# Involution on one core: products 7 and 8 of each image joined to X by transfers of their own, and the first experts' results counted exactly

## Chip, cores and metric

One core of a Trainium2 chip. The metric is device microseconds for one execution of the whole program. Three runs of the kernel before gave a median of 1173.37 us.

## The reference, cut to what matters

The program is a stack of a binary convolution, a mixture of 8 experts (two a token), an involution and a mixture of 16 experts (eight a token, with a capacity), with norms and residuals between them, on 16 images of 128 channels and 32 x 32 pixels. Two parts are touched.

The first experts (`_L0_ffn_ref`): for each token the two chosen experts, weighted and summed.

```python
for e in range(E):
    h = jax.nn.relu(x_flat @ W1[e] + b1[e])
    y = h @ W2[e] + b2[e]
    out = out + combine[:, e:e + 1] * y
```

The involution (`_L1_conv_ref`): nine taps; each is a weight per pixel, grown from the image, times the image shifted by that tap; the nine products are summed, and the sum is added to x.

```python
xv = d4_1x1(x, w_v)
pats = unfold_patches(xv, k).reshape(b, G, gc, 8, k * k, h, w)
out = (wv * pats).sum(axis=4)
...
x = x + _L1_conv_ref(_ln_c(x), ...)
```

## The kernel before

Everything is hand-scheduled: each engine has its program, written in the order in which it runs, and engines meet by semaphores alone. No planner sets an order. Phases end with all engines having reached the end of their block; a new block begins on all of them together.

**First experts** (`experts0`, lines 424 to 674). Tokens are sorted by their pair of experts into tiles of 128 rows (`SLOT`). How many tiles there are is known only at run time: VectorE works it out in `later_tables` (line 1078) and writes it to `env.totals`, and engines load it into a register with `count` (line 454). For a tile, TensorE turns the rows, multiplies them up to the 512 hidden values of each expert of the pair (line 526 and the two behind it) and down again (lines 544 to 546, eight matmuls a tile in each); ScalarE takes the rectified values in float16 (line 592), VectorE their rest (line 638). VectorE writes the result of a tile into one of 8 buffers (`OUTS`, line 658), with the token numbers beside it, and GpSimd sends it off with an indirect transfer (`send`, line 487, the transfer itself at line 489). GpSimd sends in groups of 8, so up to 7 sends behind the last real result have no rows: VectorE gives them token numbers out of bounds (line 672), for which nothing is written. The first 24 sends stand among the scatters of line 1140. The first tile begins with `take(0)` on VectorE (line 633), behind `later_tables` in VectorE's program.

**Involution** (`phase_involution`, line 1511). The images are taken one after the other; the passes of images 0, 1 and 12 to 15 are written out, those of images 2 to 11 are a loop of two (`images`, line 1553). Within a pass on image n, TensorE grows the weights of tap k into one of two PSUM buffers (`tap`, lines 1688 and 1689, four matmuls of 512 columns a tap), and among the taps it runs the steps of images n+1 and n+2: the kernels and values of the next image (lines 1669 and 1673), the group mean (1678), the turn of the rows that the first experts left (1652), the centering (1659) and the variance (1664). VectorE multiplies each grown tap by the shifted image in `product` (line 1882). Products 0 to 6 go to buffers from which GpSimd sums them with six adds (line 1628); that sum is then added to X in place by an accumulating transfer which GpSimd issues (`join_pool`, line 1616). Product 7 goes to a buffer, product 8 stays in PSUM, VectorE adds the two (`add_pair`, line 1890), and a second accumulating transfer adds this sum to X (`join_own`, line 1621); GpSimd issues it in the next image's pass, behind that image's third add. Both transfers of an image write the same part of X, so the second waits for the landing of the first:

```python
def join_own(n, q):
    pool.wait_ge(S["summed"], n * OWN_ADDS + OWN_ADDS)
    wait_apart(pool, S["pool_joined"], n * 16 + 16, env.passed)
    pool.dma_start(image(X, n), flat(own_sum[q]), accum_op=ALU.add).then_inc(S["own_joined"], 16)
```

SyncE reloads the rows of a later image (line 1569) and stores a finished image (line 1581), in turn, the store waiting for `own_joined`. VectorE's product k of an image waits until GpSimd's add k of the image before has read its buffer.

**The way into the last experts.** The choice of experts for the first two images runs on VectorE (`select`, lines 1398 to 1417), then `join_last` adds the last image's own sum to X (line 1922), then `weigh` (lines 1422 to 1432) waits for the ranks that TensorE counts. GpSimd adds its sum to the last image (line 1639), behind `join_last`, and then casts the spread weights (line 1248), which TensorE needs for the last experts.

## Time and profile before

| | |
|---|---|
| runs | 1169.5, 1173.37, 1174.52 us |
| profiled execution | 1174.4 us, span 1172.6 us, granted TensorE clock 0.958 |
| busy over the span | TensorE 1024.1, VectorE 904.3, ScalarE 778.9, GpSimd 566.7 us |
| first experts | from about 320 to 773.6 us of the span |
| involution | 773.6 to about 1084 us |
| last experts | from there to 1172.6 us |

All times in a timeline are microseconds from the first instruction of the span. A row of it gives the start, the duration, the engine, the line, the operation with output and inputs, and in brackets how long the engine had been idle and whose work ended that. An engine name with a q is its queue: an issue, or work of its sequencer. Rows of one line that follow each other are merged, with their number behind the x. "ps" is PSUM; XN, WT, Y and X are the large buffers in SBUF.

### The profile page before, as it was taken

The numbers are of one execution on the slowest core, as the hardware profiler recorded it, in microseconds if no ns is written. First come the engines' busy times: TensorE is split into PE (matmuls) and PEld (weight loads), VectorE is DVE, ScalarE is ACT, GpSimd is POOL, SyncE is SP. The second block draws the span as 40 slices with busy tenths as digits, with TensorE's granted clock in tenths as the row PEclk, the third lists the DMA queues.
The fourth block names the chain that finished last, engine by engine and source line by source line (L and its number), as shares of the span: only waits on it lengthen the run. The fifth ranks groups of instructions, "written<-read, shape, count | busy, mean of one in ns | idle before, by whom it ended". The sixth has DMA issues, their size and how long they took to land. (4 is left out here: it accounts for less than half of the span.)

```text
span 1172.6 us, 34488 instructions
## 1 busy us (share of the span) xinstructions
PE 1024.1 (87%) x9800; PEld 707.4 (60%) x9800; DVE 904.3 (77%) x2105; ACT 778.9 (66%) x2031; POOL 566.7 (48%) x442
## 2 busy tenths in 40 slices
PE   7957698898499999999999999837999999997498
PEld 2322254444299999999999999813434434433364
DVE  4669768878667777777787787706999999997687
ACT  6866399998467777777777777626656666663275
POOL 0014127657646533333333333355789889899100
PEclk9989899999789999999999999969999999999599
DMA  7200023321223211111111111121554464443000
GB/s 229 71 0 0 3 86 107 98 74 49 63 70 101 75 47 46 48 45 46 41 42 40 40 44 42 39 82 36 147 118 105 114 142 109 108 108 90 20 1 37
DMA packets 64928, 80.98 MB, mean 69 GB/s; under 512 B 10362, under 2 KB 50958, under 8 KB 64705
## 3 DMA queue, kind: packets, MB, share of 16 engines
q1 hardware_dynamic: 51552, 46.93, 13.9%
q0 software_dynamic: 13280, 32.73, 11.1%
q8 instruction: 66, 1.08, 0.4%
q14 instruction: 30, 0.24, 0.1%
HBM read 36.57 MB, written 28.88 MB: 56 GB/s over the span
## 5 line engine op out<-in xcount | busy, mean ns | idle before, releaser
L592 ACT ACTIVATE Y<-ps 128x256 f16<-128x256 f32 x584 | 223.7, 383 | 127.5 <-PE ps L546 93.8
L489 POOL DMA_INDIRECT expert_out<-Y x152 | 149.5, 983 | 273.1 <-DVE Y L658 241.6
L638 DVE SCALAR_TENSOR_TENSOR Y<-ps,Y 128x256 f16<-128x256 f32 x584 | 241.5, 422 | 45.2 <-ACT Y L592 36.6
L1628 POOL TENSOR_TENSOR XN<-XN 128x1024 f32<-128x1024 f32 x96 | 231.1, 2407 | 37.4 <-DVE XN L1882 30.8
L526 PE MATMUL ps<-Y,weights 128*128 128x128 f16 x1168 | 212.9, 220 | 6.3 <-DVE Y L638 5.8
L527 PE MATMUL ps<-Y,weights 128*128 128x128 f16 x1168 | 212.8, 220 | 0.0
L530 PE MATMUL ps<-Y,weights 128*128 128x128 f16 x1168 | 212.8, 220 | 0.0
L544 PE MATMUL ps<-weights,Y 128*128 128x128 f16 x1160 | 210.1, 220 | 0.0
L545 PE MATMUL ps<-weights,Y 128*128 128x128 f16 x1160 | 210.1, 220 | 0.0
L546 PE MATMUL ps<-weights,Y 128*128 128x128 f16 x1160 | 210.0, 219 | 0.0
L1882 DVE SCALAR_TENSOR_TENSOR XN<-ps,iv_w2b,WT 128x1024 f32<-128x1024 f32 x128 | 159.9, 1278 | 17.5 <-PE ps L1689 16.0
L1140 POOL DMA_INDIRECT dispatched<-d_rows,slot x128 | 128.2, 1002 | 91.8 <-issue 49.6
L526 PEld LDWEIGHTS ps<-Y,weights 128*128 128x128 f16 x1168 | 114.9, 98 | 11.3 <-DVE Y L638 10.4
L1688 PE MATMUL ps<-WT 128*128 128x512 f16 x288 | 109.6, 380 | 9.4 <-DVE XN L1882 5.9
L530 PEld LDWEIGHTS ps<-Y,weights 128*128 128x128 f16 x1168 | 115.1, 99 | 0.3 <-DVE Y L633 0.3
L527 PEld LDWEIGHTS ps<-Y,weights 128*128 128x128 f16 x1168 | 115.0, 98 | 0.0
L544 PEld LDWEIGHTS ps<-weights,Y 128*128 128x128 f16 x1160 | 113.9, 98 | 0.0
L545 PEld LDWEIGHTS ps<-weights,Y 128*128 128x128 f16 x1160 | 113.9, 98 | 0.0
L546 PEld LDWEIGHTS ps<-weights,Y 128*128 128x128 f16 x1160 | 113.9, 98 | 0.0
L1689 PE MATMUL ps<-WT 128*128 128x512 f16 x288 | 109.1, 379 | 0.0
L1688 PEld LDWEIGHTS ps<-WT 128*128 128x128 f16 x288 | 29.2, 101 | 69.9 <-DVE XN L1882 34.1
L549 PE MATMUL ps<-weights,ones 128*128 128x128 bf16 x290 | 63.6, 219 | 0.0
(322 smaller groups left out, 2119.8 us busy)
## 6 DMA issues: line engine op xcount, KB each, us to landing
X<-XN POOLq DMA_DIRECT2D x30, 512.0 KB, 4.5
Y<-dispatched SPq DMA_DIRECT2D x152, 65.5 KB
X<-x SPq DMA_DIRECT2D x16, 512.0 KB, 4.5
XN<-expert_out SPq DMA_DIRECT2D x16, 512.0 KB, 4.2
out<-X SPq DMA_DIRECT2D x16, 512.0 KB, 3.0
Y<-w_moe SPq DMA_DIRECT2D x8, 512.0 KB
expert_out<-Y POOLq DMA_INDIRECT x152, 2.2
dispatched<-d_rows,slot POOLq DMA_INDIRECT x128, 2.4
```

The lines of the kernel that those rows point to most:

```text
L489: pool.indirect_dma_start(env.yt, bass.IndirectOffsetOnAxis(ap=token[:, k:k + 1], axis=0), result[:, k, :], None, bounds_check=TOKENS - 1, ...
L526: pe.matmul(out, high, xh, start=True, stop=False)
L527: pe.matmul(out, low, xh, start=False, stop=False)
L530: mm = pe.matmul(out, high, xl, start=False, stop=True)
L544: pe.matmul(y[e], hh[e][:, cols], high, start=(k == 0), stop=False)
L545: pe.matmul(y[e], hh[e][:, cols], low, start=False, stop=False)
L546: mm = pe.matmul(y[e], hl[e][:, cols], high, start=False, stop=False)
L592: act.activation(hh[e][:, part_cols[h]], hidden[e][h], ACT.Relu).then_inc(hi_ready[e], 1)
L638: dve.scalar_tensor_tensor(hl[e][:, cols], hidden[e][h], 0.0, hh[e][:, cols], ALU.max, ALU.subtract).then_inc(h_split[e], 1)
L1628: pool.tensor_tensor(pool_sum[q][:, :, :], pool_part[0][:, :, :] if k == 1 else pool_sum[q][:, :, :], pool_part[k][:, :, :], ALU.add).then ...
L1688: pe.matmul(dst[:, h], wa[:, k, :], ct[q][:, h], start=True, stop=False)
L1882: dve.scalar_tensor_tensor(dst, grown, w2b[:, k:k + 1], xv[q][:, dy:dy + SIDE, dx:dx + SIDE], ALU.add, ALU.mult)\
```

## The change

It has two parts. In the involution, product 8 too is written to SBUF, both products have two buffers each (`seven`, `eight`), and each is added to X by an accumulating transfer: `join_seven` in the next pass behind the second add, `join_eight` behind the fourth. The three transfers of an image wait for each other's landing. `add_pair` and TensorE's wait for it ahead of tap 1 are gone; products 7 and 8 wait until the transfers of the image two before have landed. For the last image, VectorE adds product 7 to product 8 and that to X. ScalarE's unread outputs (lines 1797 and 1798) go to the buffers of the norm, in float32. Five semaphores of the coefficients become one.

In the first experts the number of results is split into groups of 8 and a rest of 1 to 8. The groups run as before; the rest is sent one by one from a ninth buffer, each send waiting for the landing of the one before. No send is without rows. VectorE works out the two numbers behind the tables.

The core of the diff (left out: constants, TensorE's wait for the last sum, semaphore names, the coefficients' semaphore, the size of `totals`):

```diff
@@ -438,13 +438,14 @@
     h_ready, hi_ready, h_split, y_ready = ([sem(f"m0_{n}{e}") for e in range(2)] for n in ("h_ready", "hi_ready", "h_split", "y_ready"))
     part_ready, out_ready, result_free = (sem(f"m0_{n}") for n in ("part_ready", "out_ready", "result_free"))
     stored, ready = [sem(f"m0_stored{k}") for k in range(LANDINGS)], sem("m0_ready")
+    last_stored, last_free = sem("m0_last_stored"), sem("m0_last_free")
     rows = view(RING * ROW).rearrange("p (k c) -> p k c", k=RING)
     halves = rows[:, :, :].rearrange("p k c -> p (k c)").bitcast(F16).rearrange("p (k c) -> p k c", k=RING)
     idh = view(P, F16)
     x = view(2 * P, F16).rearrange("p (k c) -> p k c", k=2)
     xh, xl = x[:, 0, :], x[:, 1, :]
     hh, hl = ([view(H0, F16) for e in range(2)] for n in ("hh", "hl"))
-    part, result, token = view(C), view(OUTS * C).rearrange("p (k c) -> p k c", k=OUTS), view(OUTS, U32)
+    part, result, token = view(C), view((OUTS + 1) * C).rearrange("p (k c) -> p k c", k=OUTS + 1), view(OUTS + 1, U32)
     hidden = [[env.psum[e][:, h * HALF:h * HALF + H0 // 2] for h in range(2)] for e in range(2)]
     y = [env.psum[2][:, e * HALF:e * HALF + C] for e in range(2)]
     turn = [env.psum[3][:, k * HALF:k * HALF + P] for k in range(2)]
@@ -497,11 +498,17 @@
 
     def experts_gpsimd(pool):
         pool.wait_ge(tables, 2)
-        groups = (count(pool, 0, ENTRIES, MAX_TILES) + OUTS - 1) // OUTS
+        groups, left = count(pool, 2, ENTRIES // OUTS - 1, MAX_TILES // OUTS), count(pool, 3, 1, OUTS)
         with pool.Fori(SENT_EARLY // OUTS, groups) as j:
             for k in range(OUTS):
                 send(pool, j, k)
-        pool.sem_inc(result_free, OUTS)
+        pool.sem_inc(last_free, 1)
+        with pool.Fori(0, left) as i:
+            wait_apart(pool, out_ready, groups * OUTS + i + RING + 1, env.passed)
+            pool.indirect_dma_start(env.yt, bass.IndirectOffsetOnAxis(ap=token[:, OUTS:OUTS + 1], axis=0), result[:, OUTS, :], None,
+                                    bounds_check=TOKENS - 1, oob_is_err=False).then_inc(last_stored, 16)
+            pool.wait_ge(last_stored, i * 16 + 16)
+            pool.sem_inc(last_free, 1)
         for k in range(LANDINGS):
             pool.wait_ge(stored[k], groups * (16 * OUTS // LANDINGS))
 
@@ -652,8 +659,12 @@
             low(i + 1, 1, 1)
             dve.wait_ge(y_ready[1], i * 2 + 2)
             dve.wait_ge(part_ready, i + 2)
-            dve.wait_ge(result_free, i + 1)
-            out = bass.ds(i % OUTS, 1)
+            if last is None:
+                dve.wait_ge(result_free, i + 1)
+                out = bass.ds(i % OUTS, 1)
+            else:
+                dve.wait_ge(last_free, last + 1)
+                out = slice(OUTS, OUTS + 1)
             dve.tensor_copy(token[:, out], gate(i, 2))
             dve.scalar_tensor_tensor(result[:, out, :].rearrange("p k c -> p (k c)"), y[1], gate(i, 1), part[:, :], ALU.mult, ALU.add)\
                .then_inc(out_ready, 1)
@@ -663,13 +674,11 @@
         with dve.Fori(0, early) as i:
             tile(i)
         dve.wait_ge(tables, 2)
-        total = count(dve, 0, ENTRIES, MAX_TILES)
-        with dve.Fori(early, total) as i:
+        groups, left = count(dve, 2, ENTRIES // OUTS - 1, MAX_TILES // OUTS), count(dve, 3, 1, OUTS)
+        with dve.Fori(early, groups * OUTS) as i:
             tile(i)
-        for k in range(OUTS - 1):
-            i = total + k
-            dve.wait_ge(result_free, i + 1)
-            dve.tensor_scalar(token[:, bass.ds(i % OUTS, 1)], env.lane, 0.0, float(TOKENS), ALU.mult, ALU.add).then_inc(out_ready, 1)
+        with dve.Fori(0, left) as i:
+            tile(groups * OUTS + i, i)
 
     return Programs(experts_sync, send, experts_gpsimd, experts_tensor, experts_scalar, prepare, experts_vector, result_free)
 
@@ -1094,6 +1103,11 @@
                 link(dve.scalar_tensor_tensor(delta2, first2, lane2, delta2, ALU.is_le, ALU.mult))
                 link(dve.tensor_reduce(table[:, 1:2], delta2, AX.X, ALU.add))
                 dve.scalar_tensor_tensor(table[:, 1:2], table[:, 1:2], lane2, inside, ALU.add, ALU.mult).then_inc(counted, 1)
+                groups, left = env.totals[:, 2:3], env.totals[:, 3:4]
+                link(dve.tensor_scalar(left, total[0:1, :], -1.0, None, ALU.add))
+                link(dve.tensor_scalar(groups, left, OUTS.bit_length() - 1, None, ALU.arith_shift_right))
+                link(dve.tensor_scalar(left, left, OUTS - 1, None, ALU.bitwise_and))
+                link(dve.tensor_scalar(left, left, 1, None, ALU.add))
 
             residual(0)
             residual(1)
@@ -1532,13 +1546,12 @@
         wa, wb = (later_wt(TAPS * P, F16).rearrange("p (k o) -> p k o", k=TAPS) for _ in range(2))
         got = [later_xn(TPI, C) for q in range(2)]
         sq, rs, y = (sb(n, [P, PIX]) for n in ("sq", "rs", "y"))
-        unread = [later_wt(PIX, F16) for k in range(2)]
         ct = [later_wt(PIX, F16) for q in range(2)]
         xv = [later_wt(PAD * PAD, F32).rearrange("p (h w) -> p h w", w=PAD) for q in range(2)]
         pool_part = [later_xn(SIDE, SIDE) for k in range(POOL_TAPS)]
         pool_sum = [later_xn(SIDE, SIDE) for q in range(2)]
-        own_part = later_xn(SIDE, SIDE)
-        own_sum = [later_xn(SIDE, SIDE) for q in range(2)]
+        seven = [later_xn(SIDE, SIDE), later_wt(PIX, F32).rearrange("p (h w) -> p h w", w=SIDE)]
+        eight = [later_xn(SIDE, SIDE) for q in range(2)]
         t = sb("t", [P, 32])
         tail = gate_experts1(nc, env, ctx, a, out, S, sq, rs, y)
         D = env.psum
@@ -1615,10 +1628,15 @@
                 wait_apart(pool, S["pool_summed"], n * POOL_ADDS + POOL_ADDS, env.passed)
                 pool.dma_start(image(X, n), flat(pool_sum[q]), accum_op=ALU.add).then_inc(S["pool_joined"], 16)
 
-            def join_own(n, q):
-                pool.wait_ge(S["summed"], n * OWN_ADDS + OWN_ADDS)
+            def join_seven(n, q):
+                pool.wait_ge(S["product_ready"], n * TAPS + POOL_TAPS + 3)
                 wait_apart(pool, S["pool_joined"], n * 16 + 16, env.passed)
-                pool.dma_start(image(X, n), flat(own_sum[q]), accum_op=ALU.add).then_inc(S["own_joined"], 16)
+                pool.dma_start(image(X, n), flat(seven[q]), accum_op=ALU.add).then_inc(S["seven_joined"], 16)
+
+            def join_eight(n, q):
+                pool.wait_ge(S["product_ready"], n * TAPS + TAPS + 2)
+                wait_apart(pool, S["seven_joined"], n * 16 + 16, env.passed)
+                pool.dma_start(image(X, n), flat(eight[q]), accum_op=ALU.add).then_inc(S["own_joined"], 16)
 
             def body(n, q, ahead):
                 for k in range(1, POOL_TAPS):
@@ -1627,14 +1645,16 @@
                         pool.wait_ge(S["pool_summed"], n * POOL_ADDS + k - 1)
                     pool.tensor_tensor(pool_sum[q][:, :, :], pool_part[0][:, :, :] if k == 1 else pool_sum[q][:, :, :],
                                        pool_part[k][:, :, :], ALU.add).then_inc(S["pool_summed"], 1)
-                    if k == 3 and (not isinstance(n, int) or n > 0):
-                        join_own(n - 1, 1 - q)
+                    if k == 2 and (not isinstance(n, int) or n > 0):
+                        join_seven(n - 1, 1 - q)
+                    if k == 4 and (not isinstance(n, int) or n > 0):
+                        join_eight(n - 1, 1 - q)
                 if not isinstance(n, int) or n < IMAGES - 1:
                     join_pool(n, q)
 
             images(pool, body)
             last = IMAGES - 1
-            pool.wait_ge(S["summed"], IMAGES * OWN_ADDS + 1)
+            pool.wait_ge(S["summed"], 2)
             pool.wait_ge(S["pool_summed"], IMAGES * POOL_ADDS)
             pool.tensor_tensor(grid(image(X, last)), grid(image(X, last)), pool_sum[last % 2][:, :, :], ALU.add).then_inc(S["pool_summed"], 1)
             tail.gpsimd[1](pool)
@@ -1680,8 +1700,6 @@
             def tap(n, q, k):
                 if k == 0:
                     pe.wait_ge(S["split_ready"], n + 2)
-                if k == 1 and (not isinstance(n, int) or n > 0):
-                    pe.wait_ge(S["summed"], n * OWN_ADDS)
                 pe.wait_ge(S["product_ready"], n * TAPS + k + 1)
                 dst = tap_out(q, k)
                 for h in halves:
@@ -1794,26 +1812,26 @@
             def moments(n):
 
                 act.wait_ge(S["t_ready"], n + 1)
-                act.activation(unread[0][:, :], D[0][:, :], ACT.Copy, scale=1.0 / PIX, accum_out=t[:, 0:1]).then_inc(S["e2_ready"], 1)
-                act.activation(unread[1][:, :], D[0][:, :], ACT.Square, scale=PIX ** -0.5, accum_out=t[:, 1:2]).then_inc(S["e2_ready"], 1)
+                act.activation(sq[:, :], D[0][:, :], ACT.Copy, scale=1.0 / PIX, accum_out=t[:, 0:1]).then_inc(S["e2_ready"], 1)
+                act.activation(rs[:, :], D[0][:, :], ACT.Square, scale=PIX ** -0.5, accum_out=t[:, 1:2]).then_inc(S["e2_ready"], 1)
...
@@ -1878,16 +1896,11 @@
                         dve.wait_ge(S["pool_summed"], n * POOL_ADDS - POOL_ADDS + max(k, 1))
                     dst = pool_part[k][:, :, :]
                 else:
-                    dst = own_part[:, :, :] if k == POOL_TAPS else grown
+                    if not isinstance(n, int) or n > 1:
+                        dve.wait_ge(S["own_joined"], n * 16 - 16)
+                    dst = (seven if k == POOL_TAPS else eight)[q]
                 dve.scalar_tensor_tensor(dst, grown, w2b[:, k:k + 1], xv[q][:, dy:dy + SIDE, dx:dx + SIDE], ALU.add, ALU.mult)\
                    .then_inc(S["product_ready"], 1)
-
-            def add_pair(n, q):
-
-                dve.wait_ge(S["product_ready"], n * TAPS + POOL_TAPS + 4)
-                if not isinstance(n, int) or n > 1:
-                    dve.wait_ge(S["own_joined"], n * 16 - 16)
-                dve.tensor_tensor(own_sum[q][:, :, :], grid(tap_out(q, POOL_TAPS + 1)[:, :]), own_part[:, :, :], ALU.add).then_inc(S["summed"], 1)
 
             def body(n, q, ahead):
                 first = isinstance(n, int) and n == 0
@@ -1905,7 +1918,6 @@
                         for h in range(2):
                             if ahead >= 2:
                                 norm(n + 2, h)
-                add_pair(n, q)
 
             for h in range(2):
                 add_x(0, h)
@@ -1918,8 +1930,11 @@
 
             def join_last():
                 last = IMAGES - 1
-                dve.wait_ge(S["summed"], IMAGES * OWN_ADDS)
-                dve.tensor_tensor(grid(image(X, last)), grid(image(X, last)), own_sum[last % 2][:, :, :], ALU.add).then_inc(S["summed"], 1)
+                q = last % 2
+                dve.wait_ge(S["product_ready"], IMAGES * TAPS + 2)
+                dve.tensor_tensor(eight[q], eight[q], seven[q], ALU.add).then_inc(S["summed"], 1)
+                dve.wait_ge(S["summed"], 1)
+                dve.tensor_tensor(grid(image(X, last)), grid(image(X, last)), eight[q], ALU.add).then_inc(S["summed"], 1)
 
             tail.vector(dve, join_last)
 
```

The places at which instructions move. In GpSimd's program at the end of the first experts, before: the loop over groups ends and the phase is over (L506).

```order
L489 DMA expert_out<-Y 16384x128
L501 ISA
L501 COMPARE_AND_BRANCH
L506 ISA
L682 UNCONDITIONAL_BRANCH
```

With the change, by its own line numbers, a loop over the rest follows, with one send at line 508 and the wait for its landing at line 510:

```order
L490 DMA expert_out<-Y 16384x128
L502 REGISTER_ALU
L502 COMPARE_AND_BRANCH
L506 UNCONDITIONAL_BRANCH
L506 ISA
L508 DMA expert_out<-Y 16384x128
L510 ISA
L506 REGISTER_ALU
L506 COMPARE_AND_BRANCH
L513 REGISTER_ALU
```

The sends in groups end with the loop; one send stands behind them in a loop of its own.

In GpSimd's program in the loop over images, one pass before: six adds (L1628), one transfer behind the third, one behind the sixth (ISA and REGISTER_ALU rows are waits and their values).

```order
L1628 TENSOR_TENSOR XN<-XN 128x1024
L99 ISA
L1621 ISA
L1621 DMA X<-XN 128x1024
L1625 REGISTER_ALU
L1627 REGISTER_ALU
L1628 TENSOR_TENSOR XN<-XN 128x1024
```

With the change: adds are L1646, and transfers stand behind the second (L1634), the fourth (L1639) and the sixth (L1629).

```order
L1634 DMA X<-WT 128x1024
L1643 REGISTER_ALU
L1645 REGISTER_ALU
L1646 TENSOR_TENSOR XN<-XN 128x1024
L1643 REGISTER_ALU
L1645 REGISTER_ALU
L1646 TENSOR_TENSOR XN<-XN 128x1024
L1637 REGISTER_ALU
L1639 DMA X<-XN 128x1024
```

A pass has three transfers in place of two, with two adds between one and the next.

In VectorE's program, the end of a pass in the loop, before: norm (L1864), product 8 into PSUM, the sum of the two products, then product 0 of the next image.

```order
L1864 TENSOR_TENSOR iv_y<-ps,iv_rs 128x512 x2
L1871 REGISTER_ALU
L1882 SCALAR_TENSOR_TENSOR ps<-ps,iv_w2b,WT 128x1024
L1887 REGISTER_ALU
L1889 ISA
L1890 TENSOR_TENSOR XN<-ps,XN 128x1024
L1871 ISA
L1873 ISA
L1878 ISA
L1882 SCALAR_TENSOR_TENSOR XN<-ps,iv_w2b,WT 128x1024
```

With the change (norm L1882, product L1902):

```order
L1882 TENSOR_TENSOR iv_y<-ps,iv_rs 128x512 x2
L1889 REGISTER_ALU
L1902 SCALAR_TENSOR_TENSOR XN<-ps,iv_w2b,WT 128x1024
L1889 ISA
L1891 ISA
L1896 ISA
L1902 SCALAR_TENSOR_TENSOR XN<-ps,iv_w2b,WT 128x1024
```

Product 0 of the next image stands directly behind product 8.

## Rows read from the trace of the kernel before

**Rows 1.** The page's costliest groups (line, engine, output and inputs | busy us, mean ns | idle)

```profile
L546 PE MATMUL ps<-weights,Y 128*128 128x128 f16 x1160 | 210.0, 219 | 0.0
```

**Rows 2.** Timeline of GpSimd at the end of the first experts

```profile
760.52 0.98 POOL L489 DMA_INDIRECT expert_out<-Y  x1 [1.92 <-DVE Y L672]
...
769.52 0.98 POOL L489 DMA_INDIRECT expert_out<-Y  x1 [0.30 <-issue]
773.67 1.80 POOL L1240 MEMSET g_parts<- 128x2048 bf16 x1 [3.16 <-POOLq L682]
```

**Rows 3.** The sends of line 489: from issue to landing

```profile
DMA to landing us min/median/max: 2.1/2.2/3.9
```

**Rows 4.** Timeline of GpSimd in the image loop

```profile
946.15 0.86 POOL L1616 DMA_DIRECT2D X<-XN  x1 [0.69 <-POOL XN L1628]
947.66 7.22 POOL L1628 TENSOR_TENSOR XN<-XN 128x1024 f32<-128x1024 f32 x3 [0.65 <-DVE XN L1882]
954.83 0.86 POOL L1621 DMA_DIRECT2D X<-XN  x1
955.42 7.55 POOL L1628 TENSOR_TENSOR XN<-XN 128x1024 f32<-128x1024 f32 x3
963.65 0.86 POOL L1616 DMA_DIRECT2D X<-XN  x1 [0.68 <-POOL XN L1628]
```

**Rows 5.** Timeline of VectorE at the start of the first experts

```profile
318.19 0.16 DVE L1046 SCALAR_TENSOR_TENSOR r_hit<-r_l,r_hit 1x14 f32<-1x14 f32 x1
318.38 0.16 DVE L1047 TENSOR_SCALAR words<-r_hit 1x14 int32<-1x14 f32 x1
...
320.05 0.28 DVE L633 CAST Y<-ps 127x128 f16<-127x128 f32 x1
```

**Rows 6.** Timeline of VectorE in the image loop

```profile
961.31 1.22 DVE L1890 TENSOR_TENSOR XN<-ps,XN 128x1024 f32<-128x1024 f32 x1
```

**Rows 7.** Timeline of TensorE in the image loop: the end of tap 1, the start of tap 2

```profile
945.87 0.38 PE L1689 MATMUL ps<-WT 128*128 128x512 f16 x1
946.30 0.39 PE L1688 MATMUL ps<-WT 128*128 128x512 f16 x1
```

**Rows 8.** Timeline of TensorE: tap 1 of the last image

```profile
1064.29 0.38 PE L1688 MATMUL ps<-WT 128*128 128x512 f16 x1 [1.42 <-DVE XN L1890]
```

**Rows 9.** Timeline of GpSimd from the last images on

```profile
1051.18 0.86 POOL L1616 DMA_DIRECT2D X<-XN  x1 [0.60 <-POOL XN L1628]
...
1068.45 0.86 POOL L1616 DMA_DIRECT2D X<-XN  x1 [0.61 <-POOL XN L1628]
...
1077.23 7.67 POOL L1628 TENSOR_TENSOR XN<-XN 128x1024 f32<-128x1024 f32 x3
1095.85 2.34 POOL L1639 TENSOR_TENSOR X<-X,XN 128x1024 f32<-128x1024 f32 x1 [10.94 <-DVE X L1922]
1098.13 1.23 POOL L1248 CAST spread<-spread 128x1024 bf16<-128x1024 f32 x1
```

**Rows 10.** The accumulating transfers of line 1616: from issue to landing

```profile
DMA to landing us min/median/max: 4.5/4.5/5.7
```

**Rows 11.** Timeline of SyncE's queue in the image loop

```profile
960.47 0.39 SPq L1569 DMA_DIRECT2D XN<-expert_out  x1
```

**Rows 12.** Timeline of VectorE: product 6 of the last image

```profile
1077.52 1.28 DVE L1882 SCALAR_TENSOR_TENSOR XN<-ps,iv_w2b,WT 128x1024 f32<-128x1024 f32 x1 [1.75 <-PE ps L1689]
```

**Rows 13.** Timeline of VectorE from the choice of experts on

```profile
1088.99 0.43 DVE L1400 TENSOR_TENSOR g_biased<-g_scores,g_gate_b 128x256 f32<-128x256 f32 x1
...
1094.54 1.23 DVE L1922 TENSOR_TENSOR X<-X,XN 128x1024 f32<-128x1024 f32 x1
1096.38 0.29 DVE L1422 SCALAR_TENSOR_TENSOR g_keep<-ps,g_total 128x128 f32<-128x128 f32 x1 [0.61 <-PE ps L1277]
1096.70 1.76 DVE L1425 TENSOR_TENSOR g_biased<-g_masked,g_keep 128x256 f32<-128x256 f32 x1
1098.50 1.01 DVE L1428 CAST g_parts<-g_biased 128x256 bf16<-128x256 f32 x1
```

32 lines of the change are left out of this document (16 added, 16 removed).

## The prediction

> **What bounds the kernel now.** I read the times, then the busy shares by stretch, then the timeline of each engine at the three places that the diff touches, and last the landing times of the transfers. The sum is made against the profiled execution, 1174.4 us with a span of 1172.6, 1.0 above the median of the runs (1173.4). What a measurement here can tell from no change is 0.5%, 5.9 us.
>
> The first experts: 1160 matmuls of line 546, 8 a tile, make 145 real results, and the line has no idle time before it, so TensorE sets the pace [rows 1]. At their end GpSimd is alone: the send of the last real result starts at 760.52, seven empty ones follow 1.285 apart, the last at 769.52, and the next phase starts at 773.67 [rows 2]. In the involution a pass over an image is 17.50 us (from one GpSimd transfer of line 1616, at 946.15, to the next, at 963.65 [rows 4]). There TensorE, VectorE and GpSimd are all close to full, so I cost each alone.
>
> **Part 1, the count of results.** 145 is 18 groups of 8 and 1 left: no empty send is issued, and the one left over waits for no transfer but its own. The seven steps of 1.285 go: **-9.0**. The last send lands in the same 2.2 us [rows 3] as an empty one, and the 2 us of phase change behind it stay. Nothing else is late behind GpSimd: no other engine has work in that stretch. The left-over tile runs a copy of the code of its own; I give it nothing, with up to +1 as a bound, from the 2 us that the change of phase, which is new code too, takes. The price of knowing the numbers is four linked small operations in later_tables. Such steps follow each other by 0.19 us (318.19, 318.38 [rows 5]), so the cast of line 633, at 320.05, comes up to 0.76 later. The third matmul of the first tile waits for it. A few tenths may be hidden; TensorE is the bound from there on, so the rest stays: **+0.6**.
>
> **Part 2, the image loop on VectorE and TensorE.** The sum of two products goes, 1.22 us at 961.31, ahead of the next product 0 [rows 6]. That isn't 1.22 us of time. Products 1 to 3 wait for taps, and ahead of tap 1 TensorE runs six float32 matmuls on the norm's y, so tap 1 ends at 946.25 whether product 0 came early or not. What goes is the wait of tap 2 for product 0: it started at 946.30 and could start at 946.08, 0.216 behind the matmul at 945.87 [rows 7]. All behind it moves up by 0.22: ten passes in the loop, and about half of that in the unrolled ones, 2.5 us. The last image gives more: its tap 1 waited 1.42 us for the sum [rows 8], and now waits for product 8 alone, 1.3 earlier. VectorE and TensorE alone would end 3.8 us sooner. TensorE's wait for the sum, which is taken out, is the same microseconds.
>
> **Part 3, the image loop on GpSimd.** Here a transfer is added. In a pass GpSimd does six adds and two issues, and waits: behind line 1616 the next add starts 1.51 us after the issue (946.15 to 947.66), behind line 1621 only 0.59 (954.83 to 955.42), so 0.92 us is a wait for VectorE. A block of three adds behind an issue takes 7.55 instead of 7.23, 0.32 longer [rows 4]. GpSimd's own need is 17.50 - 0.92 + 0.32 = 16.90. One more issue costs the 7.76 from 947.66 to 955.42 less 7.30 for three adds and a gap, 0.46, and the 0.32: 0.78. The new pass is 17.68, above the 17.50 of now and the 17.3 that the others would take. **GpSimd becomes the bound.** Unrolled blocks take 7.67 in place of 7.55; a pass needs about 17.86 there, against 17.27 now (1051.18 to 1068.45 [rows 9]).
>
> The transfers on X stand in a chain: each waits for the landing of the one before. Line 1616 comes 0.68 behind the add that it waits for [rows 4]; an issue that waits for a landing has about that on top too. From issue to issue lie 0.59 and two adds, some 5.7 us. At the median landing of 4.5 nothing is lost; at the slowest, 5.7 [rows 10], 0.65. SyncE's reload of 512 KB, at 960.47 [rows 11], comes 3.2 us ahead of line 1616 now; afterwards it is released by the later landing and comes some 1 us ahead, so the two overlap. I take 0.1 a pass in the loop, near the median, which is also the minimum.
>
> GpSimd's last add ends at 1084.90 now (1077.23 + 7.67 [rows 9]). It moves by 1.1 in image 1 (0.78, and 0.3 because its transfers meet the loads of the last experts' weights), ten loop passes at 0.18 + 0.10, three unrolled at 0.55, and 0.78 in the last image: +6.3, to 1091.2. VectorE may run ahead by one image's parts: product 6 of the last image, at 1077.52 now [rows 12] and wanted at 1073.7, needs the last add of the image before, which ended 0.6 ahead of 1068.45 [rows 9] and will at about 1073.3. So VectorE is just free.
>
> Who waits for GpSimd then? Today it sits idle 10.94 us ahead of line 1639 [rows 9], and the choice of experts on VectorE (lines 1398 to 1417) runs in that gap. It won't be a gap any more. Beside GpSimd's two operations at 1095.85 and 1098.13 [rows 9] the product of line 1425 took 1.76 us, where line 1400, of the same shape, took 0.43, and ended 0.27 behind the first; the cast of line 1428 took 1.01 and ended 0.15 behind the second. Line 1422, with an operand in PSUM, took 0.29 beside the same add [rows 13]. So a VectorE operation with all operands in SBUF is held until GpSimd's is over. The choice would begin nearly 4 us sooner, and its steps of lines 1398, 1400 and 1403 each meet an add; line 1403 gets through behind the last add, which one of them pushes to 1091.6. From line 1403 to the end of the choice is 5.1 us (1088.99 + 0.43 to 1094.54 [rows 13]), so it ends at 1096.7, not at 1094.5: **+2.2**, where VectorE alone promised -3.8. If the reciprocal of line 1399 is held too, it is 1.8 more.
>
> The Trainium skill ("SBUF — State Buffer", Who interferes with whom) says that a VectorE operation with two SBUF inputs, or in a two-port mode, and a GpSimd operation that reads SBUF exclude each other for a whole instruction, and that one with a single SBUF input outside those modes doesn't. By that the reciprocal runs free and the sum stays as it is. The Trainium skill ("DMA: Bandwidth & Descriptors", Anatomy of one DMA) fits a GpSimd transfer as 2.0 us + bytes/436e3, an estimated 3.2 us for these 512 KB; the trace has 4.5. By 3.2 no landing would ever be waited for, and the time would be an estimated 1.3 us less.
>
> **Part 4, the end.** join_last is now two adds in place of one. The one at 1094.54 fitted in the wait for the ranks (0.61 idle ahead of line 1422); the second doesn't, by 0.7. But it also starts line 1639 1.25 later, for which line 1425 is held, and the cast behind it: **+1.25** [rows 13]. TensorE needs the spread weights of line 1248 only after the ranks, the weights' transposes and the table of finals, so its delay is covered. ScalarE's outputs in float32 in place of float16, the shared semaphore of the coefficients and the other buffers cost nothing: ScalarE waits for TensorE on both sides of them.
>
> **Sum:** 0.6 - 9.0 + 2.2 + 1.25 = -4.95, or 1169.4 in the profiled frame; against the median **1168.4 us**.
>
> **Rivals.** *The gap stays a gap.* GpSimd's adds come a little quicker, or the small operations aren't held. Then VectorE's -3.8 shows: 0.6 - 9.0 - 3.8 + 1.25 = -10.95, 1162.4 us. For it: GpSimd's new pass is only 0.18 above the old. Against: the 1.76 us of line 1425.
> *The chain of transfers is the bound (slower).* All landings of an image queue with reloads, stores and each other. Its place is the two waits in join_seven and join_eight, with GpSimd's adds queued behind them; each costs up to 0.65. With both at that price in 14 passes it is +18.2 less the 1.0 already counted: 1185.6. From 0.45 a pass on the gain is gone; from about 0.85 on it is slower by over 0.5%. For it: one landing of line 1616 took 5.7. Against: its median is 4.5 [rows 10].
> *The seven sends were cover.* Something else ends the first experts, such as SyncE's last fetches or the fetch of new code: no -9.0, 1177.4 us. Against: nothing but GpSimd works between 762 and 773.
>
> **How the numbers follow.** GpSimd as the bound 0.64, over 1165 to 1172 (0.25 us a pass either way); the gap stays 0.20; the chain of transfers 0.10, half of it short of its full price; the sends as cover 0.06. The range 1162 to 1176 leaves out half of the first rival, most of the second and the third: under 0.2. Faster by over 0.5% is below 1167.5: the first rival and a third of the main case, 0.42. Slower, above 1179.2, is the chain near its full price, 0.06. Within 0.5%: 0.52.
>
> **What would show it.** Right: the next phase starts near 765; line 1616's successor comes every 17.7 to 17.9 us in the loop, with no idle time behind it; GpSimd's last add ends within a microsecond of the third step of the choice; the successors of lines 1400 and 1403 take over 1 us. Wrong: a period of 17.3 (the first rival); idle time of GpSimd ahead of the new issues, ended by a landing (the second); a stretch from the last real send to the next phase as long as now (the third).

## The result, and the profile after

The changed kernel takes **1176.4 us** (median of 20 runs), the kernel before 1172.8 beside it: a ratio of 1.0033, 95% interval 1.0023 to 1.0043. One of the 20 runs took 5805.1 us, in the slow state, and is left out of the ratio; the median of the other 19 is 1176.3. The kernel is 3.6 us slower, where the forecast had it 5 us faster; the time lies just above the forecast's range of 1162 to 1176. The profiled execution took 1178.9 us with a span of 1177.1, 4.5 more than before.

The first product of the involution starts at 792.24, 7.50 us earlier than before (799.74). What lies behind it is counted from there, since the stretch ahead of it moved by up to 3 us between profiled executions of kernels that are the same up to that point. The column "forecast" is the prediction's 1091.6, 1096.7 and its two terms behind them, less 799.74:

| from the first product to | before | forecast | after |
|---|---|---|---|
| the end of GpSimd's last add of products | 285.2 | 291.9 | 301.1 |
| the end of the choice of experts | 294.8 | 297.0 | 306.0 |
| the end of the weights of the choice | 301.3 | 304.8 | 313.8 |

The forecast lay within a microsecond up to the involution, missed 9.2 us in it, and was right behind it.

The end of the first experts, timeline of GpSimd in the changed kernel; columns as in [rows 2]:

```profile
759.18 0.98 POOL L490 DMA_INDIRECT expert_out<-Y  x1 [1.93 <-DVE Y L669]
761.83 0.98 POOL L508 DMA_INDIRECT expert_out<-Y  x1 [1.67 <-DVE Y L669]
766.00 1.80 POOL L1254 MEMSET g_parts<- 128x2048 bf16 x1 [3.18 <-POOLq L691]
```

There is one send, of the tile left over, and the next phase starts 4.17 us behind it, as it stood 4.15 behind the last of eight before. The seven steps are gone.

The image loop, timeline of GpSimd:

```profile
928.41 0.86 POOL L1629 DMA_DIRECT2D X<-XN  x1 [0.68 <-POOL XN L1646]
929.01 5.10 POOL L1646 TENSOR_TENSOR XN<-XN 128x1024 f32<-128x1024 f32 x2
935.03 0.87 POOL L1634 DMA_DIRECT2D X<-XN  x1 [0.92 <-DVE XN L1902]
935.63 5.12 POOL L1646 TENSOR_TENSOR XN<-XN 128x1024 f32<-128x1024 f32 x2
940.68 0.87 POOL L1639 DMA_DIRECT2D X<-XN  x1
941.27 5.10 POOL L1646 TENSOR_TENSOR XN<-XN 128x1024 f32<-128x1024 f32 x2
947.05 0.87 POOL L1629 DMA_DIRECT2D X<-XN  x1 [0.68 <-POOL XN L1646]
947.65 5.12 POOL L1646 TENSOR_TENSOR XN<-XN 128x1024 f32<-128x1024 f32 x2
954.22 0.86 POOL L1634 DMA_DIRECT2D X<-WT  x1 [1.45 <-DVE XN L1902]
```

A pass takes 18.64 us (928.41 to 947.05), not 17.68. All of the surplus is the idle time ahead of line 1634, the first of the two new transfers: 0.92 here, 1.45 in the next pass. The releaser printed is VectorE's product, done long before; in six other passes the profile names the transfer. In all, ten passes wait there (image 2 and images 4 to 12), 0.80 to 1.45 us each, 10.0 together. The answer for line 1629:

```profile
  POOL X L1634: 5.6, 6
DMA to landing us min/median/max: 4.5/6.0/6.5
```

Its landings took 6.0 us in the middle, where those of [rows 10] took 4.5. Line 1634 waits for that landing. What runs beside it is on SyncE's queue, both released by the landing of the transfer of line 1639:

```profile
945.44 0.35 SPq L1594 DMA_DIRECT2D out<-X  x1
946.19 0.39 SPq L1582 DMA_DIRECT2D XN<-expert_out  x1
```

The store starts 1.6 us and the reload 0.9 us ahead of the transfer at 947.05. In the kernel before, the reload started 3.1 to 3.4 us ahead of it and had about 1 us still to run, and the store had landed.

The choice of experts, timeline of VectorE, then of GpSimd:

```profile
1087.11 0.72 DVE L1412 TENSOR_SCALAR g_scores<-g_scores 128x256 f32<-128x256 f32 x1 [4.98 <-ACT g_scores L1362]
1087.87 1.75 DVE L1413 RECIPROCAL g_scores<-g_scores 128x256 f32<-128x256 f32 x1
1089.66 1.49 DVE L1414 TENSOR_TENSOR g_biased<-g_scores,g_gate_b 128x256 f32<-128x256 f32 x1
1091.18 2.31 DVE L1417 TENSOR_TENSOR g_group<-g_biased 128x128 f32<-128x128 f32 x1
...
1098.28 1.22 DVE L1935 TENSOR_TENSOR XN<-XN,WT 128x1024 f32<-128x1024 f32 x1
1099.54 1.22 DVE L1937 TENSOR_TENSOR X<-X,XN 128x1024 f32<-128x1024 f32 x1
1100.69 0.28 DVE L1436 SCALAR_TENSOR_TENSOR g_keep<-ps,g_total 128x128 f32<-128x128 f32 x1
1101.00 2.46 DVE L1439 TENSOR_TENSOR g_biased<-g_masked,g_keep 128x256 f32<-128x256 f32 x1
```

```profile
1088.22 5.12 POOL L1646 TENSOR_TENSOR XN<-XN 128x1024 f32<-128x1024 f32 x2
1100.85 2.34 POOL L1659 TENSOR_TENSOR X<-X,XN 128x1024 f32<-128x1024 f32 x1 [7.50 <-DVE X L1937]
```

All four steps have their operands in SBUF alone. Lines 1412, 1414 and 1417 are longer than the 0.29, 0.42 and 0.29 us that they take where GpSimd is idle (e1 below), and the reciprocal keeps its 1.75. Line 1417 ends at 1093.49, 0.15 behind GpSimd's last add (1093.34). That is the place at which GpSimd's delay becomes the kernel's.

### The profile page after: what moved, and what is told of

The parts are those of the page before. It is cut to its first block and busy times, and to the rows that moved or that the text cites. A ratio compares the mean times of both kernels' runs of the same rounds, so it can differ in the third digit from the quotient of the medians.

```text
span 1177.1 us, 34527 instructions
## 1 busy us (share of the span) xinstructions
PE 1025.8 (87%) x9800; PEld 710.1 (60%) x9800; DVE 884.9 (75%) x2087; ACT 778.7 (66%) x2031; POOL 574.4 (49%) x450
## 5 line engine op out<-in xcount | busy, mean ns | idle before, releaser
L490 POOL DMA_INDIRECT expert_out<-Y x144 | 141.8, 985 | 270.5 <-DVE Y L669 243.3
L1646 POOL TENSOR_TENSOR XN<-XN 128x1024 f32<-128x1024 f32 x96 | 239.8, 2498 | 28.6 <-DVE XN L1902 23.5
L1902 DVE SCALAR_TENSOR_TENSOR XN<-ps,iv_w2b,WT 128x1024 f32<-128x1024 f32 x136 | 169.9, 1279 | 42.5 <-PE ps L1707 33.1
L669 DVE SCALAR_TENSOR_TENSOR Y<-ps,Y 128x128 f32 (+1 forms) x145 | 50.8, 351 | 24.1 <-issue 17.2
```

Of the source, the lines that this page charges most:

```text
L490: pool.indirect_dma_start(env.yt, bass.IndirectOffsetOnAxis(ap=token[:, k:k + 1], axis=0), result[:, k, :], None, bounds_check=TOKENS - 1, ...
L1646: pool.tensor_tensor(pool_sum[q][:, :, :], pool_part[0][:, :, :] if k == 1 else pool_sum[q][:, :, :], pool_part[k][:, :, :], ALU.add).then ...
L1902: dve.scalar_tensor_tensor(dst, grown, w2b[:, k:k + 1], xv[q][:, dy:dy + SIDE, dx:dx + SIDE], ALU.add, ALU.mult)\
```

## The experiments

Each kernel was timed in five rounds against the kernel before, whose median was 1172.7 to 1173.1 us beside them. "Last add" and "choice" are counted from the first product, as above; "pass" is GpSimd's, from one transfer of the sum of seven to the next, the middle value over images 4 to 11.

| kernel | us | ratio to before, 95% | pass | last add | choice |
|---|---|---|---|---|---|
| before | 1172.8 | 1 | 17.49 | 285.2 | 294.8 |
| after | 1176.4 | 1.0023 to 1.0043 | 18.66 | 301.1 | 306.0 |
| e1, count alone | 1166.0 | 0.9928 to 0.9954 | 17.50 | 285.3 | 294.8 |
| e2, joins alone | 1183.6 | 1.0078 to 1.0107 | 18.51 | 299.0 | 304.0 |
| e3, joins apart | 1170.3 | 0.9968 to 0.9988 | 17.65 | 294.5 | 299.4 |
| e4, SyncE moved | 1168.8 | 0.9952 to 0.9978 | 17.63 | 291.9 | 296.8 |
| e9, store beside | 1168.3 | 0.9950 to 0.9978 | 17.63 | 291.7 | 296.6 |
| e10, reload beside | 1168.6 | 0.9957 to 0.9977 | 17.65 | 292.2 | 297.1 |
| e5, joins late | 1165.0 | 0.9919 to 0.9951 | 16.79 | 283.8 | 292.8 |
| e6, seven early | 1161.3 | 0.9881 to 0.9925 | 16.79 | 284.2 | 292.8 |
| e11, SyncE back | 1180.0 | 1.0045 to 1.0074 | 19.08 | 305.4 | 310.8 |
| e12, port cleared | 1162.9 | 0.9901 to 0.9939 | 16.79 | 283.9 | 292.6 |
| e7, bound loaded | 1167.5 | 0.9936 to 0.9971 | 17.49 | 285.3 | 297.1 |
| e8, port held | 1168.8 | 0.9949 to 0.9976 | 17.49 | 285.3 | 297.3 |

**The two halves of the change.** e1 takes the part of the change in the first experts, e2 that in the involution ("the joins", the transfers that add to X).

> Only the first half of the change: the exact number of results in the first experts, with its four small operations in the tables; the involution keeps the sum of two products on VectorE and its two transfers an image. (ScalarE's shared semaphore and buffers are taken over too, since they free the semaphores that the count needs.) Theory 1, that the seven empty sends stood alone on the path and the rest of the kernel only shifts: in the trace of after the next phase starts 7.7 us earlier (765.99 for 773.67) and the first product of the involution 7.5 earlier; nothing behind it changes, so the time is 7.5 us below before, 1165.3 us, and the involution's pass stays at 17.50 us. Rival, that part of the gain is lost again behind the phase (a clock drop that comes at another place, transfers that meet): 1168 or more.

> Only the second half: products 7 and 8 each by an accumulating transfer of its own, two adds in join_last; the first experts as before, with their seven empty sends. Theory 1: the whole loss sits here. The change as a whole is 3.6 us slower though 7.5 are gained ahead of the involution, so this part costs 11.1: 1183.9 us, with GpSimd's pass in the loop at 18.6 us. Rival, that the two parts work on each other (the involution is slower only because it starts 7.5 us earlier, at another state of the clock): 1178 or less.

Measured: 1166.0 and 1183.6. The count gains 6.8 us, the joins cost 10.8, and the sum of the two, +4.0, is what the whole change shows, +3.6, within the intervals. So the halves do not work on each other, as far as the times tell, and the loss is in the involution alone.

**The wait for the landing**: once the wait is given room (e3), once the landing is made faster (e4).

```diff
-                    if k == 2 and (not isinstance(n, int) or n > 0):
+                    if k == 3 and (not isinstance(n, int) or n > 0):
                         join_seven(n - 1, 1 - q)
-                    if k == 4 and (not isinstance(n, int) or n > 0):
+                    if k == 5 and (not isinstance(n, int) or n > 0):
                         join_eight(n - 1, 1 - q)
```

> The changed kernel, with the two new transfers issued behind the third and the fifth add of an image in place of the second and the fourth. Between the transfer of line 1629 and the next one then lie three adds, some 8.2 us, more than its landing of 6.0 to 6.5 needs; the next two lie as far apart as now, and the third has no one waiting. Nothing else is changed. Theory 1, that GpSimd loses its time to the wait for that landing (0.9 to 1.45 us idle ahead of line 1634 in ten passes): the idle time goes, a pass is 17.7 us in place of 18.6, GpSimd's last add ends 9 to 10 us earlier, and so does the kernel: 1167 us, where the forecast had it. Rival 1, that GpSimd's pass is long by its own instructions (a third issue, adds that are slower behind an issue): no wait is saved, 1176 us. Rival 2, that the wait moves to the second transfer, whose landing then meets the reload: 1172 us or more, with idle time ahead of line 1639.

The core of e4's edit (left out: the bounds of SyncE's loop and the stores and reloads that move out of it):

```diff
                 for q in range(2):
+                    sp.wait_ge(S["seven_joined"], (n + q) * 16 - 32)
+                    send(n + q - 4)
                     reload(n + q, q)
-                    send(n + q - 2)
```

> The changed kernel, with SyncE's store and reload moved: in the loop both are released by the landing of product 7's transfer instead of product 8's (the store is that of the image before, whose sum has landed by then), so that they run beside the third transfer, for which nobody waits, and not beside that of line 1629. GpSimd's program is untouched. Theory 1, that line 1629 lands in 6.0 us instead of 4.5 because the reload of 512 KB and the store go at the same time: it lands in 4.5 again, the idle time ahead of line 1634 goes, a pass is 17.7 us, and the time is 1167 us, as with the transfers set apart. Rival, that the landing is slow for another reason (it follows an add at once, or two transfers on X meet): landings stay at 6.0 and the time at 1176 us.

Measured: 1170.3 and 1168.8. In e3 the landings in the loop still take 6.0, and nobody waits for them; in e4 they take 4.5. Both passes are near 17.65: the wait was the surplus, and its cause is what SyncE runs beside the transfer. The third transfer pays instead: in e4 it lands in 7.0 us, and nobody waits for it. e3 misses its 1167 for a reason that was not expected: in image 1 line 1639 waits 4.99 us, because there line 1634's transfer meets the loads of the last experts' weights and lands 10.2 us after its issue; so its last add comes 2.6 us behind that of e4. e4's last add ends 291.9 behind the first product and its choice at 296.8, the forecast's 291.9 and 297.0. That they agree to 0.2 is in part luck: e4 still waits 0.88 us for a landing in image 2 and 0.69 in image 11, where the forecast counted 0.1 in each of ten passes.

**Store or reload?** In SyncE's program e9 moves the reload alone, e10 the store alone (in e10 the loop waits for `own_joined`, reloads, waits for `seven_joined`, stores).

> The changed kernel with only SyncE's reload moved beside the third transfer; the store stays where it is, released by the landing of product 8's transfer and so beside that of line 1629. Theory 1, that the reload of 512 KB in 1024 packets is what makes line 1629's transfer land late: it lands in 4.5 us, GpSimd's pass is 17.65 us, the time as with both moved, 1168.8 us. Rival 1, that the store does it: the landing stays at 6.0, the time at 1176.4 us. Rival 2, that both share it: a landing of about 5.2 us, with 0.3 us of idle time a pass, 1171 to 1173 us.

> The reverse: only SyncE's store moved beside the third transfer, the reload stays beside that of line 1629. Theory 1 (the reload makes the landing late): 6.0 us, idle time of 0.9 to 1.4 us ahead of the next issue, 1176 us as the changed kernel. Rival 1 (the store does it): 4.5 us and 1168.8 us. Rival 2 (both): about 5.2 us, 1171 to 1173 us.

Measured: 1168.3 and 1168.6, neither 1176 nor 1171 to 1173: neither version costs anything that the times tell. The landings of the transfer of the sum of seven between 860 and 1030 us, in e4, e9, e10 and the changed kernel, in this order:

```profile
DMA to landing us min/median/max: 4.5/4.5/4.6
```

```profile
DMA to landing us min/median/max: 4.5/4.9/5.4
```

```profile
DMA to landing us min/median/max: 4.5/5.0/5.3
```

```profile
DMA to landing us min/median/max: 5.9/6.0/6.5
```

From issue to issue there are 5.64 us, and an issue that waits comes 0.6 to 0.7 behind the landing: 5.0 is free, 6.0 costs 1.

These two runs do not tell how much of the 6.0 each neighbour has, since the one that stayed did not keep its distance. The changed kernel has the store 1.6 to 1.7 us and the reload 0.6 to 0.9 ahead of the transfer. In e9 the third transfer lands later, so the store comes up to 0.7 ahead; in e10 the reload is the first in SyncE's queue and comes 1.2 to 1.6 ahead. The third transfer of these kernels says more. From 890 to 1000 us it has one neighbour alone, in e9 the reload, 0.8 to 0.9 ahead, and in e10 the store, 0.5 to 0.9 ahead (lines 1644 and 1643):

```profile
DMA to landing us min/median/max: 5.4/5.7/5.9
```

```profile
DMA to landing us min/median/max: 4.6/4.6/4.9
```

With the store alone 1.8 ahead, in two passes of e9, the transfer of the sum of seven took 4.5. So the reload, at the distance of the changed kernel, makes 5.7 of the 4.5 by itself, which is most of the surplus, and the store alone, at 1.8 and so near its distance, adds nothing. The theory of both expectations is nearer to the truth than their times suggest; a run with the reload alone 0.6 to 0.9 us ahead of line 1629 was not made.

**GpSimd free again, and a faster kernel.** e5 is e4 with the three transfers each one add later, so that none waits for the add just ahead of it (SyncE's part, as in e4, is left out):

```diff
+                    if k == 1 and (not isinstance(n, int) or n > 0):
+                        join_pool(n - 1, 1 - q)
-                    if k == 2 and (not isinstance(n, int) or n > 0):
+                    if k == 3 and (not isinstance(n, int) or n > 0):
                         join_seven(n - 1, 1 - q)
-                    if k == 4 and (not isinstance(n, int) or n > 0):
+                    if k == 5 and (not isinstance(n, int) or n > 0):
...
-                if not isinstance(n, int) or n < IMAGES - 1:
-                    join_pool(n, q)
```

> The kernel with SyncE moved, and the three transfers of an image each issued one add later: the sum of seven behind the first add of the next image, product 7 behind the third, product 8 behind the fifth. Each transfer then follows an add that doesn't feed it, so the 0.68 us from GpSimd's own last add to the issue goes. Theory: GpSimd's need is 17.65 less 0.68, 16.97 us, below the 17.27 that TensorE and VectorE take without the sum; the pass falls to 17.27, GpSimd is free again, the choice starts behind VectorE's last product and its steps are not held. Against the count alone (1166.0) that is 3.8 us won in the loop and 1.25 lost in join_last: 1163.4 us. Rival: the 0.68 is no wait that can be hidden, or a landing is waited for at the new place; GpSimd stays the bound at 17.6, 1168.8 us as now.

Measured: 1165.0. GpSimd's pass is 16.79 while it catches up, VectorE's and TensorE's 17.27 all along, and VectorE's last product ends 280.0 behind the first, as it does in e4, where before it was 283.9. That is the forecast's gain of 3.8 for these two engines, and here GpSimd's last add, at 283.8, no longer hides it. The steps of the choice are short again. Yet the choice ends only 2.0 us earlier than in e1, and that is TensorE's clock. The matmuls of the router, in e1 and then in e5:

```profile
1074.89 3.72 PE L1279 MATMUL ps<-g_gate_w,XN 128*128 128x16 f32 x32 [1.20 <-DVE XN L1396]
```

```profile
1068.82 5.66 PE L1279 MATMUL ps<-g_gate_w,XN 128*128 128x16 f32 x32 [1.20 <-DVE XN L1396]
```

In e1 the granted clock falls from 1.0 to 0.5 (2.4 to 1.2 GHz) at 1079.12, behind them; in e5 at 1070.27, when they are 1.45 us under way. Counted from the first product, they start 4.0 us earlier than in e1, and the clock falls 6.7 earlier. That takes back 1.9 of the 4.0.

In e6 product 7 of the last image goes to X ahead of the choice, and `join_last` has one add again (its first add, of product 7 to product 8, is taken out):

```diff
+            dve.wait_ge(S["product_ready"], IMAGES * TAPS + 2)
+            dve.tensor_tensor(grid(image(X, IMAGES - 1)), grid(image(X, IMAGES - 1)), seven[(IMAGES - 1) % 2], ALU.add).then_inc(S["summed"], 1)
             tail.vector(dve, join_last)
```

> As the run before in this batch, and the last image's product 7 is added to X ahead of the choice, in the time in which VectorE waits for ScalarE's exponentials, so that join_last is one add again (product 8 to X). Theory: the 1.25 us that the second add cost behind the choice goes, 1.25 us below that run, 1162.2 us. Rival: the early add has all its operands in SBUF and meets GpSimd's last adds; it is held for up to 2.5 us, the first step of the choice comes later than ScalarE allows, and nothing or less than nothing is won.

Measured: 1161.3, the fastest of all, a ratio of 0.9903 to before. By the trace the weights of the choice end 299.4 behind the first product instead of 300.6, so the second add was worth 1.2; the rest of the 3.6 between the two medians is not told apart from chance, since their intervals overlap. The early add took 2.00 us instead of 1.22, held as the rival had it, but ScalarE still had VectorE waiting 3.13.

e11 is e6 with SyncE's loop as in the changed kernel.

> The fastest version so far (the transfers each one add later, product 7 of the last image early, 1161.3 us) with SyncE's store and reload put back to where the changed kernel has them. Theory: the store and the reload, released by product 8's landing, now meet the transfer of the sum of seven again, which lands in 6.0 us; between its issue and the next lie 5.7 to 5.9 us, of which an issue that waits for a landing wants 0.7 behind it, so about 0.9 us a pass is waited and GpSimd's need goes from 16.8 to 17.7, above the 17.27 of the others: 3 to 5 us longer, 1164 to 1166 us. Rival: the new places leave room enough, no difference, 1161.3 us.

Measured: 1180.0, far above both. Timeline of GpSimd; here line 1629 transfers the sum of seven and line 1634 waits for it:

```profile
953.23 1.17 POOL L1629 DMA_DIRECT2D X<-XN  x1
953.82 5.40 POOL L1646 TENSOR_TENSOR XN<-XN 128x1024 f32<-128x1024 f32 x2
961.63 0.86 POOL L1634 DMA_DIRECT2D X<-WT  x1 [2.40 <-DMA X<-XN]
```

```profile
DMA to landing us min/median/max: 4.8/7.6/8.3
```

The store goes at 952.75, the reload at 953.50: all three within 0.8 us, and the landing takes 7.6 where 6.0 was expected. Of that, 0.3 is the issue itself (1.17 us long in place of 0.86); with it and no neighbour the landing takes 4.8 in e6. The gain of the late joins rests on SyncE's place.

**The hold of VectorE by GpSimd.** e8 is e1 with three more adds behind GpSimd's last one, which nobody waits for:

```diff
+            for k in range(3):
+                pool.tensor_tensor(pool_part[k][:, :, :], pool_part[k][:, :, :], pool_part[k + 3][:, :, :], ALU.add).then_inc(S["border"], 1)
```

> The exact count alone (1166.0 us), with three more adds of 128x1024 on GpSimd behind its last one, on buffers that nobody reads any more; nobody waits for them, and GpSimd's next real operation has 10.85 us of idle time ahead of it, so its own path is not longer. Theory 1, that an operation of VectorE with all operands in SBUF is held while GpSimd's runs: lines 1412, 1414 and 1417 of the choice, 0.29, 0.42 and 0.29 us long now, fall into that time, take over 1 us each, line 1413 (the reciprocal) keeps its 1.75, and the time is 2 to 4 us longer, 1168 to 1170 us. Rival, that the long steps of the choice in the changed kernel had another cause: the three steps keep their durations and the time stays at 1166.0 us.

Measured: 1168.8, 2.8 above e1. Timeline of VectorE in e8:

```profile
1079.14 0.59 DVE L1412 TENSOR_SCALAR g_scores<-g_scores 128x256 f32<-128x256 f32 x1 [1.97 <-ACT g_scores L1362]
1079.77 1.75 DVE L1413 RECIPROCAL g_scores<-g_scores 128x256 f32<-128x256 f32 x1
1081.55 0.66 DVE L1414 TENSOR_TENSOR g_biased<-g_scores,g_gate_b 128x256 f32<-128x256 f32 x1
1082.25 2.31 DVE L1417 TENSOR_TENSOR g_group<-g_biased 128x128 f32<-128x128 f32 x1
```

Lines 1412, 1414 and 1417 take 0.30, 0.24 and 2.02 more than in e1, 2.56 in all; the reciprocal takes nothing more. Only the third took over 1 us: how long a step is held depends on where in an add it begins. The Trainium skill ("SBUF — State Buffer", Who interferes with whom) says that an operation with two SBUF inputs, or one in a two-port mode, and one of GpSimd that reads SBUF exclude each other for a whole instruction. These rows agree for lines 1414 and 1417, with two SBUF inputs, and for the reciprocal, with one. Line 1412 has one too and was held; by that page it would have to run in a two-port mode, and no row shows the mode.

e12 is e6 with GpSimd's cast of the spread weights behind its last product add and its add to X behind the weights of the choice.

> The fastest version so far (1161.3 us), with GpSimd's last two operations taken out of VectorE's way: the cast of the spread weights right behind GpSimd's last add of products, and the add of the sum of seven to X only once VectorE has worked out the weights of the choice. Theory: lines 1439 and 1442, 1.76 and 1.01 us beside those two operations, take 0.43 and 0.29 again; line 1412 may be held by the cast for 0.3 at most. That is 1.7 to 2.0 us, 1159.4 us. Rival 1: the last image's sum, 5 us later now, is waited for (by its store, or by the next phase), and the gain is lost. Rival 2: the two steps are long for another reason and stay so, 1161.3 us.

Measured: 1162.9, no difference from e6 that the intervals tell. The theory's 1159.4 did not come, and neither rival named the reason. Lines 1439 and 1442 did fall to 0.43 and 0.29 us, as the theory had it. But GpSimd's add to X now meets the next step (timeline of VectorE, then of GpSimd):

```profile
1085.84 0.43 DVE L1439 TENSOR_TENSOR g_biased<-g_masked,g_keep 128x256 f32<-128x256 f32 x1
1086.30 0.29 DVE L1442 CAST g_parts<-g_biased 128x256 bf16<-128x256 f32 x1
...
1088.09 2.32 DVE L1450 COPY g_short<-g_need 128x8 f32<-128x8 f32 x1
```

```profile
1087.99 2.39 POOL L1664 TENSOR_TENSOR X<-X,XN 128x1024 f32<-128x1024 f32 x1 [12.03 <-DVEq L1459]
```

A copy of 8 columns takes 2.32 us, in e6 0.16: the hold was moved, not removed. It took back 2.2 of the 2.3 us by which the weights of the choice came earlier (297.1 for 299.4), and TensorE's first matmul of the last experts started 302.9 behind the first product, in e6 303.5. Then the clock took that back: the granted clock rose to 1.0 only 314.8 behind the first product, in e6 at 307.7, and a pair of line 1321's matmuls takes 1.06 us below it and 0.60 above. The profiled execution of e12 ends 371.4 behind the first product, that of e6 369.1.

**The drift of the tiles.** In the second tile loop of the first experts VectorE's step from line 668 to 669 has a gap of 0.22 us where it had 0.10, and from 545 to 755 us TensorE waits 5.6 us at the turns of its own loop for line 645, where it waited 4.4. Before and after:

```profile
646.33 0.35 DVE L658 SCALAR_TENSOR_TENSOR Y<-ps,Y 128x128 f32 x1
```

```profile
647.21 0.35 DVE L669 SCALAR_TENSOR_TENSOR Y<-ps,Y 128x128 f32 x1 [0.22 <-issue]
```

e7 takes the product `groups * OUTS` out of VectorE's registers (left out: the table's third number becomes eight times the number of groups, and GpSimd divides it):

```diff
-        with dve.Fori(early, groups * OUTS) as i:
+        with dve.Fori(early, whole) as i:
```

> The exact count alone (1166.0 us), but the table holds the number of results in whole groups itself, eight times the number of groups, so that VectorE's loop bound is a loaded value and not a product in a register; again four small operations. Theory: the 0.12 us more between lines 668 and 669 in each tile of that loop, and with it the 1.0 us by which the tiles drift behind those of before, come from the register work of that bound; both go, 1165.0 us. Rival: they come from something else in the new code (the loop's place, the waits), the gap stays at 0.215 and the time at 1166.0 us.

Measured: 1167.5, and the gap is still 0.22 (the expectation's 0.215); the theory fell. The register instructions between the two lines are the same in number and kind before and after. What makes the gap stays open. Why e7's median is 1.5 us above e1's stays open too: their intervals overlap, and e7's profiled execution, at 1163.3 us, was the fastest of its six, although there the clock fell 1.1 us into the router's matmuls, which took 5.98 us.

## Why the prediction was wrong

**Part 1, -9.0 and +0.6: right but for 0.9 us.** The seven steps are gone, the 4.15 behind the last send stayed, as forecast, and e1 keeps the gain to the end. The +0.6 for the tables came out as next to nothing, since TensorE's stop for the cast (0.32) is made up within some tiles. In its place, entering the second tile loop took 0.6 more, the drift above another 1.1 over its tiles, and the last tile came 0.2 sooner: together 1.5. The remainder's copy of the tile was given a bound of +1; the cost came up in the loop beside it.

**Part 2, VectorE and TensorE alone: right.** The pass is 17.27 (forecast 17.3), the last product ends 3.9 us earlier (forecast 3.8) once GpSimd is out of the way. In the changed kernel itself it holds for six passes; then VectorE, one image's parts ahead, runs into GpSimd.

**Part 3, GpSimd: the mechanism right, one term mis-sized.** "GpSimd becomes the bound" held, and its own need is 17.65 (forecast 17.68). The failed step is the sentence "I take 0.1 a pass in the loop, near the median, which is also the minimum". The forecast itself said that SyncE's reload would overlap with the transfer, and then priced the landing by [rows 10]. In the loop of that kernel the reload started 3.1 to 3.4 us ahead and had about 1 us still to run, and the landing took 4.5; started 0.6 to 0.9 us ahead, with the store 1.6 to 1.7, it made 6.0. Ten passes waited ahead of line 1634, 10.0 us in all, where 1.0 was counted; nine of them, from 872.20 to 1040.72, took 18.72 each, 1.07 above GpSimd's need. That is 9.0 of the 9.2 by which the last add was late; the other 0.2 is what is left of small differences both ways, 0.5 more in image 1 the largest. The upper end of that very row, 5.7, would have given 0.65; the truth lay above it, and the row held no case with both neighbours so near. The Trainium skill ("DMA: Bandwidth & Descriptors", Anatomy of one DMA) with its estimated 3.2 us is further off: no landing of these transfers took under 4.5. The forecast named the reload alone, and the third transfer of e9 bears it out: 5.7 with the reload alone 0.8 us ahead, which ahead of line 1634 would cost about 0.65 (an estimate by the same working). The store, released by the same landing a microsecond earlier, was left out; both together make the 6.0.

**The hold: right in kind and size.** The choice ends 4.9 us behind the last add in the changed kernel and in e4 (forecast 297.0 less 291.9, 5.1), and e8 shows the hold without any wait.

**Part 4, +1.25: right.** From the start of `join_last` to the end of the weights it took 6.5 us before and 7.8 after; taking the second add out gave back 1.2.

**The rivals.** The second, "the chain of transfers is the bound", is what came, but at one of its two waits: join_seven's cost about 1.0 in each of ten passes, 10.0 in all, as 0.71 in each of its fourteen would be, and join_eight's cost nothing in the loop. It put the point from which the gain is gone at 0.45 a pass, and e4 (faster) and the changed kernel (slower) lie on either side of it; its chance of 0.10 was too low, because "its median is 4.5" was held against it, a row of a kernel in which SyncE's reload met this transfer for 1 us only. The third, the sends as cover, is refuted by e1. The first is e5: 1165.0 where it said 1162.4, and of the 2.6 between them 1.9 is the clock in the router.

## What to carry to other kernels

When an edit moves the moment at which a transfer starts, its landing time must be priced with the neighbours that it will have, not by the median of a trace in which they hardly met; and the question is then how far the wait is from the point at which it is covered, since here a landing 0.5 us longer cost nothing and one 1.5 us longer cost 1. A queue released by the same semaphore that starts the next transfer is such a neighbour: releasing SyncE one transfer earlier gave back 7.6 us for a few moved lines. And an engine that nobody waits for can still delay the path by holding VectorE's steps; shifting such work a few microseconds moves the hold to the next step.

## What was not expected of the hardware

- How long an accumulating transfer of 512 KB takes to land hangs on when its neighbours of 512 KB start, and on which they are: 4.5 us alone or with the reload 3.1 us or more ahead; 5.0 with the reload 1.5 ahead and 5.7 with it 0.8 ahead; 4.5 with the store 1.8 ahead, 4.6 with it 0.8 ahead and 4.9 with it 0.5 ahead; 6.0 with the store 1.7 and the reload 0.6 to 0.9 ahead; 7.0 with the store 0.9 and the reload 0.2 ahead (e4); 7.6 with both within 0.8 us of it (e11).
- An issue costs GpSimd more than its own time: the first add behind it takes 2.66 us, any other 2.36.
- The copy of 128x8 elements on VectorE took 2.32 us beside one add of GpSimd, and 0.16 without it.
- The granted clock of TensorE falls at a moment that shifts by microseconds between kernels, and the 32 small matmuls of the router take 3.72 us where it falls behind them (before, e1, e8) and 3.8 to 6.2 where it falls within them (all others).
